# Two feed-forward stages rewritten as pipelines, and the order of work moved in one attention and in both transformers

## The chip, the cores and the metric

The kernel runs on one core of one Trainium2 chip. The metric is the device time of one execution in microseconds (us). The core has five engines that run side by side and wait for each other only through semaphores: TensorE (PE: matmuls and transposes; PEld is its weight load), VectorE (DVE), ScalarE (ACT), GpSimd (POOL) and SyncE (SP, which issues the transfers). TensorE's granted clock has two levels, 1.2 and 2.4 GHz; a granted clock of 1.00 in a row is 2.4 GHz, 0.50 is 1.2 GHz.

## The reference

`x` is 4 sequences of 512 tokens with 128 channels in float32. Four layers do

```
xn = layernorm(x);  s = attention_i(xn);  g = silu(ffn_i(xn));  x = x + s * g
```

with another attention and another feed-forward in each. Five of these eight parts are touched:

```
ffn0:  xq = fp4(xn); h = silu(xq @ fp4(Wgate).T) * (xq @ fp4(Wup).T);  y = fp4(h) @ fp4(Wdown).T     (hidden 352)
       fp4: in blocks of 16, scale = max|v| / 6, |v| / scale rounded to 0, .5, 1, 1.5, 2, 3, 4, 6, sign, * scale
attn1: 16 heads of 64, causal softmax(q k^T / 64) v, projection and bias
ffn1:  a = silu(x W1 s1) * (x W2 s2); b = gelu(a H1 s); c = gelu(b H2 s); y = c W3 s3                (hidden 512)
ffn2:  a transformer of 6 layers, 16 heads of 64, local windows of 32 keys, gated GELU of hidden 341
ffn3:  a transformer of 2 layers, 8 heads of 64, local windows of 64 keys, gated GELU of hidden 341
```

Tokens are handled in 16 tiles of 128 (TILES; four tiles, TPB, are a sequence).

## The kernel before

The program is a row of stages with a barrier of all engines between them: load, norm, attn0, ffn0, norm, attn1, ffn1, norm, attn2, ffn2, norm, attn3, ffn3, end. Inside a stage each engine has a written-out list of instructions, and the order in each list is the order of the work; nothing overtakes within an engine.

**ffn0 (`ffn0`, L1328).** One block loads the weights into `wgu` and `wd`, copies them into `src`, and rounds them: `round_fp4` (L1359) is a chain of 14 VectorE instructions, each of which waits for the one before (`step`). ScalarE first makes `mag` (absolute value) and `sgn` (sign). TensorE then transposes the rounded weights. Then a loop in hardware runs over the 4 sequences, with a barrier and a clearing of semaphores after each. In one pass everything follows in one line: copy xn to `src`, magnitude and sign, 14 steps on 512 columns, transposes, gate and up matmuls for 4 tiles with Silu and a product, magnitude and sign of 1408 columns, 14 steps on them, 12 transposes, copies, 12 matmuls of the down product, 4 copies to `u`. GpSimd only clears a tile at the start.

**attn1 (`attention1`, L1521).** 32 units (4 sequences, 8 pairs of heads). TensorE's list is `order` (L1561): for each n it holds the scores of unit n+1 (tiles 3, 2, 1, 0), between them the transposes `p` of unit n, then `weigh(n-1)` (the product of weights and values), `R(n-1)` (transposes of the reciprocal sums), the q, k and v projections of later units, and `out(n-2)`. `p`, `R`, `q`, `k`, `v` share two PSUM banks T in turn: each claims the bank that the job two before it has left (`claim`). `score(n+1, 1)` waits for the exponentials of tile 3 of the same unit, as both lie in the same banks of A. ScalarE's list (L1740) has `turned(n, 0)` ahead of `exps(n+1, 3)`.

**ffn1 (`ffn1`, L1834).** One block loads all weights and scales and waits for all ten transfers; then a hardware loop over the 4 sequences: GpSimd copies a sequence to `xb`; 8 matmuls "first" (L1885, L1886), Silu and a product; 16 matmuls "second" (L1893) and Gelu; 16 "third" and Gelu; 16 of 128 columns "last" (L1898); 4 products into `u` (L1922). A float32 matmul shows as two records.

**The transformers (`transformer`, L198).** `slots()` yields one slot for each group of 8 heads of a tile, so ffn2 (NG = 2) has 192 of them, two for a tile, and ffn3 (NG = 1) has 32, one for a tile; a slot holds work of several stages of the pipeline: `now` (attention of a group), `turn` (transposes of the next group's q and k), `ahead` (projection and norm of q, k, v), `tail` (mix the heads of a tile, and its norm), `ffn` (its gate, up, Gelu, down), `last` (its residual). For NG = 2 a slot has either `tail` and `last` or `ffn`, in turn; these are called tail slots and ffn slots below. For NG = 1 each slot has all of them. TensorE's list in a slot is: score, project q, the transpose of the norm, project k, turn p0, project v, turn p1, mix_heads, gate_up, [q here if the slot has no ffn], weigh, [q here if it has], transpose of the residual (L571), turn k, turn o, down. ScalarE's is: exponentials and squares, copy p0, copy p1, load the Gelu table, Gelu, load the Exp table, copy q (L644), copy k, copy v, copy o. The transposes and gate and up share two banks T in turn in the order of `T_list` (L235): p0, p1, gate, up, q, k, o, so q waits until Gelu has read gate, and o waits until q is copied. VectorE rotates q and k in L706 (`roped`), multiplies gate by up in L720 (`hT`), then divides the attention output (L726, L728), then norms (L680), and adds the down product to the residual in L689 at the start of the next slot. GpSimd does the powers (L398, L401) and the products of the rotation (L409 to L411).

Of the kernel before, what the change touches and what calls it, by code (L numbers as in the profile page):

```python
# [13 lines left out]
ALU = mybir.AluOpType  # L14
# [183 lines left out]
def transformer(nc, g, dram, name, depth, heads, window, hid, wqkv, qs, ks, wo, ln_g, ln_b, w1, b1, w2, b2):  # L198
# [32 lines left out]
    for now, turn, ahead, tail, ffn, last in slots():  # L231
# [10 lines left out]
    with Stage(nc, name) as st:  # L242
# [97 lines left out]
        with nc.Block() as block:  # L340
# [73 lines left out]
            def _(pe):  # L414
# [124 lines left out]
                for now, turn, ahead, tail, ffn, last in slots():  # L539
# [26 lines left out]
                    if turn is not None and ffn is not None:  # L566
                        turn_qk("q", turn)
# [12 lines left out]
            def _(act):  # L580
# [28 lines left out]

                def copy_v(n):  # L610
# [3 lines left out]
                for now, turn, ahead, tail, ffn, last in slots():  # L614
# [25 lines left out]
                    if ahead is not None and ffn is None:  # L640
                        copy_v(ahead)
                    if turn is not None:
                        t, gi = divmod(turn, NG)
                        act.activation(qT[:, turn % 2].rearrange("p j k -> p (j k)"), turned("q", turn), ACT.Copy).then_inc(T_in.sem, 1)  # L644
# [683 lines left out]
def ffn0(nc, g, d):  # L1328

    HID, BL = 352, 16  # L1330
    HC = [(c, min(P, HID - c)) for c in range(0, HID, P)]
    u, ident, xn = g["u"], g["ident"], g["xn"]
    MAXN = TPB * HID
    with Stage(nc, "f0") as st:
        wgu = st.sb("wgu", [P, 2, len(HC), DIM])
        wd = st.sb("wd", [P, HID])
        wguT = st.sb("wguT", [P, 2, HID])
        wdT = st.sb("wdT", [P, len(HC), DIM])
        src = st.sb("src", [P, MAXN])
        mag = st.sb("mag", [P, MAXN])  # L1340
        sgn = st.sb("sgn", [P, MAXN])
        acc = st.sb("acc", [P, MAXN])
        low = st.sb("low", [P, MAXN])
        scale = st.sb("scale", [P, MAXN // BL])
        inverse = st.sb("inverse", [P, MAXN // BL])
        xqT = st.sb("xqT", [P, SEQ])
        sil = st.sb("sil", [P, 2, HID])
        hqT = st.sb("hqT", [P, len(HC), SEQ])
# [1589 lines left out]
```

## Time and profile before

| | us |
|---|---|
| runs (3), median | 4454.21 (4452.24 to 4461.76) |
| the profiled execution | 4464.67 |
| its span, first to last instruction | 4463.0 |
| ffn0, from the first instruction at 301.41 to 545.62 | 244 |
| attn1, 566 to 1034.6 | 469 |
| ffn1, 1036.05 to 1230.67 | 195 |
| ffn2, about 1761 to 3834 | 2073 |
| ffn3, about 3987 to 4445 | 458 |

The rows below come from the profiled execution. Busy time of an engine is the sum of its instructions in a stretch; the text in square brackets behind a row is how long the engine had stood idle before it and what it waited for.

### The profile page before, as it was taken

The numbers are of one execution on the slowest core, as the hardware profiler recorded it, in microseconds if no ns is written. First come the engines' busy times: TensorE is split into PE (matmuls) and PEld (weight loads), VectorE is DVE, ScalarE is ACT, GpSimd is POOL, SyncE is SP. The second block draws the span as 40 slices with busy tenths as digits, with TensorE's granted clock in tenths as the row PEclk, the third lists the DMA queues.
The fourth block names the chain that finished last, engine by engine and source line by source line (L and its number), as shares of the span: only waits on it lengthen the run. The fifth ranks groups of instructions, "written<-read, shape, count | busy, mean of one in ns | idle before, by whom it ended". The sixth has DMA issues, their size and how long they took to land. (4 is left out here: it accounts for less than half of the span.)

```text
span 4463.0 us, 101112 instructions
## 1 busy us (share of the span) xinstructions
PE 3750.9 (84%) x40099; PEld 2554.7 (57%) x40109; DVE 2919.9 (65%) x6557; ACT 2452.5 (55%) x5024; POOL 2271.0 (51%) x2200
## 2 busy tenths in 40 slices
PE   7962378887879998999999999999999999658886
PEld 4542245553446564666666666666666666556665
DVE  3335544441046564888888888888888888528885
ACT  2221145552235454666766666676667667526775
POOL 1000000000012122988888888888888888227773
PEclk9975589999979898999999999999999999779998
DMA  0000000000000001211211211211211111111010
GB/s 19 2 7 0 0 21 1 1 1 27 0 7 2 1 2 34 65 39 42 62 42 40 64 39 41 66 38 42 63 41 38 42 42 38 31 49 38 21 23 20
DMA packets 103241, 128.41 MB, mean 29 GB/s; under 512 B 38232, under 2 KB 55680, under 8 KB 101888
## 3 DMA queue, kind: packets, MB, share of 16 engines
q1 hardware_dynamic: 102784, 122.05, 10.2%
q8 instruction: 320, 5.24, 0.5%
q14 instruction: 137, 1.12, 0.1%
HBM read 31.95 MB, written 3.54 MB: 8 GB/s over the span
## 5 line engine op out<-in xcount | busy, mean ns | idle before, releaser
L398 POOL TENSOR_TENSOR t_inv<-t_ssq,half 128x8 f32<-128x8 f32 x448 | 779.6, 1743 | 94.9 <-DVE t_ssq L673 75.0
L449 PE MATMUL t_wa<-t_w_qkv,t_resid 128*128 128x512 f32 x1344 | 693.3, 615 | 60.2 <-DMA t_b<-in_L_ffn_b 56.6
L409 POOL TENSOR_TENSOR t_ra<-t_qn,t_rot 128x512 f32<-128x512 f32 x448 | 569.6, 1271 | 84.5 <-DVE t_qn L680 75.8
L598 ACT ACTIVATE t_p<-t_p 128x384 f32<-128x384 f32 (+1 forms) x448 | 241.6, 539 | 498.7 <-DVE t_p L697 489.7
L706 DVE TENSOR_TENSOR t_ra<-t_ra,t_rb 128x512 f32<-128x512 f32 x448 | 314.1, 723 | 119.1 <-POOL t_rb L411 118.9
L478 PEld LDWEIGHTS t_T<-ident,t_p 128*96 128x96 f32 (+1 forms) x1792 | 192.5, 129 | 312.4 <-ACT t_p L598 280.0
L410 POOL TENSOR_TENSOR t_rb<-t_qn,t_rot 128x256 f32<-128x256 f32 x448 | 363.7, 812 | 0.0
L411 POOL TENSOR_TENSOR t_rb<-t_qn,t_rot 128x256 f32<-128x256 f32 x448 | 338.0, 754 | 0.0
L449 PEld LDWEIGHTS t_wa<-t_w_qkv,t_resid 128*128 128x128 f32 x1344 | 212.3, 192 | 178.9 <-issue 148.9
L671 DVE TENSOR_REDUCE t_ssq<-t_sq 128x8 f32<-128x512 f32 x448 | 304.9, 681 | 13.6 <-ACT t_sq L590 10.1
L486 PE MATMUL t_T<-ident,t_ra 128*128 128x128 f32 x1792 | 268.7, 278 | 42.2 <-ACT t_gg L637 32.1
L478 PE MATMUL t_T<-ident,t_p 128*96 128x128 f32 (+1 forms) x1792 | 281.5, 280 | 17.1 <-ACT t_p L598 13.8
L680 DVE TENSOR_TENSOR t_qn<-t_wa,t_inv 128x512 f32<-128x512 f32 x448 | 290.7, 684 | 4.5 <-POOL t_inv L398 4.3
L2250 POOL TENSOR_SCALAR_AFFINE_SELECT a_pt<-a_pt 128x512 f32<-128x512 f32 x128 | 80.0, 637 | 400.8 <-ACT a_pt L2234 400.8
L2257 DVE TENSOR_REDUCE a_nmax<-a_A 128x2 f32<-128x1024 f32 (+3 forms) x256 | 205.4, 823 | 117.9 <-PE a_A L2170 115.6
L695 DVE TENSOR_REDUCE t_nmax<-t_S 128x4 f32<-128x384 f32 (+1 forms) x448 | 255.4, 570 | 39.4 <-PE t_S L469 39.4
L590 ACT ACTIVATE t_sq<-t_wa 128x512 f32<-128x512 f32 x448 | 261.5, 584 | 29.3 <-PE t_wa L449 29.3
L697 DVE TENSOR_TENSOR t_p<-t_S,t_nmax 128x384 f32<-128x384 f32 (+1 forms) x448 | 258.4, 577 | 15.4
L608 ACT ACTIVATE t_pT<-t_T 96x512 f32<-96x512 f32 (+1 forms) x448 | 263.2, 588 | 3.4 <-PE t_T L478 2.7
L496 PE MATMUL t_S<-t_v,t_pT 96*64 96x66 f32 (+1 forms) x6656 | 258.2, 225 | 0.0
L2234 ACT ACTIVATE a_pt<-a_B 128x512 f32<-128x512 f32 (+1 forms) x384 | 175.9, 528 | 143.0 <-PE a_B L2181 142.9
L496 PEld LDWEIGHTS t_S<-t_v,t_pT 96*64 96x64 f32 (+1 forms) x6656 | 227.1, 137 | 36.0 <-issue 36.0
(414 smaller groups left out, 8382.2 us busy)
## 6 DMA issues: line engine op xcount, KB each, us to landing
t_v<-t_vn SPq DMA_DIRECT2D x192, 198.0 KB, 2.6
t_v<-t_vn SPq DMA_DIRECT2D x248, 132.0 KB, 2.4
t_v<-t_vn SPq DMA_DIRECT2D x144, 66.0 KB, 1.9
t_w_qkv<-in_L_ffn_Wqkv SPq DMA_DIRECT2D x6, 1536.0 KB
t_v<-t_nothing SPq DMA_DIRECT2D x48, 66.0 KB, 1.9
t_w_o<-in_L_ffn_Wo SPq DMA_DIRECT2D x6, 512.0 KB
f_h<-t_L_ffn_h_w SPq DMA_DIRECT2D x2, 1024.0 KB, 8.1
t_w<-in_L_ffn_W SPq DMA_DIRECT2D x6, 341.0 KB
```

Of the source, the lines that this page charges most:

```text
L398: pool.tensor_tensor(inv[:, n % 2, r, :], ssq[:, n % 2, r, :], g["half"][:, 0:8], ALU.pow).then_inc(inved.sem, 1)
L409: pool.tensor_tensor(ra[:, n % 2, r], qn[:, r], spread(cos, 1, 8), ALU.mult).then_inc(cosd.sem, 1)
L410: pool.tensor_tensor(rb[:, n % 2, r, :, 0:32], qn[:, r, :, 32:64], spread(sin[:, 0:32], 1, 8), ALU.mult).then_inc(sind.sem, 1)
L411: pool.tensor_tensor(rb[:, n % 2, r, :, 32:64], qn[:, r, :, 0:32], spread(sin[:, 32:64], 1, 8), ALU.mult).then_inc(sind.sem, 1)
L449: pe.matmul(bank, resid[:, b, lo:lo + P], w_qkv[:, l % 2, at:at + 512], start=True, stop=True).then_inc(wa_up.sem, 1)
L478: m = pe.transpose(bank[0:KEYS, j * P:(j + 1) * P], p[:, r, j, :], ident[:, :])
L486: m = pe.transpose(bank[:, j * P:(j + 1) * P], ra[:, n % 2, r, 2 * j:2 * j + 2, :].rearrange("p h d -> p (h d)"), ident[:, :])
L496: m = pe.matmul(S[64 * b:64 * b + 64, r, j * VD:(j + 1) * VD], pT[0:KEYS, r, j, 64 * b:64 * b + 64], windows[b][0:KEYS, 2 * j + r, :], sta ...
L608: act.activation(pT[0:KEYS, r].rearrange("p h k -> p (h k)"), turned(f"p{r}", G)[0:KEYS], ACT.Copy).then_inc(T_in.sem, 1)
L671: v.tensor_reduce(ssq[:, n % 2, r, :], sq[:, r], X, ALU.add).then_inc(summed.sem, 1)
L680: v.tensor_tensor(qn[:, r], wa[:, wa_job[kind, n] % 3, :].rearrange("p (h d) -> p h d", h=8), spread(inv[:, n % 2, r, :], 2, HD), ALU.mult ...
L706: v.tensor_tensor(ra[:, turn % 2, r], ra[:, turn % 2, r], rb[:, turn % 2, r], ALU.add).then_inc(roped.sem, 1)
```

## The change

- ffn0 is written anew as one block. All values to be rounded lie in one tile A, and are rounded in 14 parts: x0, x1, the gate and up weights, the down weights, x2, x3, and h0 to h7 of two tiles each. VectorE does seven instructions for each part, GpSimd the last two (`subtract`, and the product with the scale). ScalarE's Abs and Sign are gone. No part waits for the one before except by the order of an engine.
- ffn1 is one block without a loop. The three kinds of hidden product of two sequences are interleaved (`order`), all PSUM banks form a ring of 8, the copy to `xb` is gone, each wait for weights is only for those used, and `u` is written once for a sequence.
- attn1: `weigh(n-1)` goes from behind the last p transposes to a place behind the first two; on ScalarE `exps(n+1, 3)` goes ahead of `turned(n, 0)`.
- Transformers: in slots with ffn the transposes of q go ahead of gate and up on TensorE, with the banks in the order p0, p1, q, gate, up, k, o; the copy of q goes ahead of the Gelu table load on ScalarE. Where NG > 1 (ffn2) `down` goes ahead of `turn_o`.

```diff
@@ transformer
-        for kind, n in (("p0", now), ("p1", now), ("gate", ffn), ("up", ffn), ("q", turn), ("k", turn), ("o", now)):
+        for kind, n in (("p0", now), ("p1", now), ("q", turn), ("gate", ffn), ("up", ffn), ("k", turn), ("o", now)):
...
                         mix_heads(tail)
+                    if turn is not None:
+                        turn_qk("q", turn)
                     if ffn is not None:
                         gate_up(ffn)
-                    if turn is not None and ffn is None:
-                        turn_qk("q", turn)
                     if now is not None:
                         weigh(now, 0)
                         weigh(now, 1)
-                    if turn is not None and ffn is not None:
-                        turn_qk("q", turn)
...
                         turn_qk("k", turn)
+                    if ffn is not None and NG > 1:
+                        down(ffn)
                     if now is not None:
                         turn_o(now)
-                    if ffn is not None:
+                    if ffn is not None and NG == 1:
                         down(ffn)
@@ ScalarE
                         copy_p(now, 1)
+                    if turn is not None and ffn is not None:
+                        copy_q(turn)
                     if ffn is not None:
 
                         act.activation(spare[:, 0:1], g["half"][0:1, 0:1], ACT.Gelu)
...
                         copy_v(ahead)
+                    if turn is not None and ffn is None:
+                        copy_q(turn)
@@ ffn0, VectorE and GpSimd, for each part (lo, size)
+                    step(v.tensor_reduce(sc, blocks(src), X, ALU.max, apply_absolute_value=True))
+                    step(v.tensor_scalar(sc, sc, 1.0 / 6.0, 1e-12, ALU.mult, ALU.max))
+                    step(v.reciprocal(inv, sc))
+                    step(v.tensor_tensor(blocks(a), blocks(src), spread(inv, 2, BL), ALU.mult))
+                    step(v.tensor_scalar(c.bitcast(U32), a.bitcast(U32), 0x7F800000, None, ALU.bitwise_and))
+                    step(v.tensor_scalar(c, c, 1.0, 1.5 * 2.0 ** 22, ALU.max, ALU.mult))
+                    v.scalar_tensor_tensor(out=a, in0=a, scalar=1.0 - 2.0 ** -24, in1=c, op0=ALU.mult, op1=ALU.add).then_inc(shifted.sem, 1)
...
+                    pool.wait_ge(shifted.sem, shifted.at(k))
+                    pool.tensor_tensor(a, a, c, ALU.subtract).then_inc(lessened.sem, 1)
+                    pool.wait_ge(lessened.sem, lessened.at(k))
+                    pool.tensor_tensor(blocks(a), blocks(a), spread(scale[:, lo // BL:(lo + size) // BL], 2, BL), ALU.mult).then_inc(rounded.sem, 1)
...
+                turn_x(0)
+                turn_gu(0)
+                turn_gu(1)
+                gate_up(0)
+                turn_d()
+                turn_x(1)
+                gate_up(1)
+                for k in range(UNITS):
+                    if k in (1, 3):
+                        turn_x((k + 3) // 2)
+                    if k + 2 < UNITS:
+                        gate_up(k + 2)
+                    turn_h(k)
+                    down(k)
@@ attention1
                 order += [("p", n, 0), ("p", n, 1)]
+            if 0 <= n - 1 < UNITS:
+                order.append(("weigh", n - 1, 0))
             if 0 <= n + 1 < UNITS:
                 order.append(("score", n + 1, 1))
...
-                order += [("weigh", n - 1, 0), ("R", n - 1, 0)]
+                order.append(("R", n - 1, 0))
...
+                    if 0 <= n + 1 < UNITS:
+                        exps(n + 1, 3)
                     if 0 <= n < UNITS:
                         turned(n, 0)
                     if 0 <= n + 1 < UNITS:
-                        exps(n + 1, 3)
                         exps(n + 1, 2)
@@ ffn1
+    order = [("first", 0), ("first", 1), ("second", 0), ("second", 1), ("third", 0), ("third", 1), ("first", 2), ("last", 0),
+             ("first", 3), ("last", 1), ("second", 2), ("second", 3), ("third", 2), ("third", 3), ("last", 2), ("last", 3)]
...
+                sp.dma_start(w1[:, :], d["t_L1_ffn_w1_w"]).then_inc(w_in, 16)
+                sp.dma_start(w2[:, :], d["t_L1_ffn_w2_w"]).then_inc(w_in, 16)
                 for k, name in enumerate(("w1", "w2", "h1", "h2")):
...
+                sp.dma_start(h1[:, :, :], d["t_L1_ffn_h1_w"].rearrange("(c p) n -> p c n", p=P)).then_inc(h1_in, 16)
+                sp.dma_start(h2[:, :, :], d["t_L1_ffn_h2_w"].rearrange("(c p) n -> p c n", p=P)).then_inc(h2_in, 16)
...
+                def claim(job):
+
+                    m = job_of[job]
+                    if m >= 8:
+                        kind, b, c = jobs[m - 8]
+                        done = {"first1": silued, "first2": gated, "second": gelu1, "third": gelu2, "last": y_in}[kind]
+                        pe.wait_ge(done.sem, done.at(b, c + 1))
+                    return bank[:, m % 8, :]
...
+            @block.scalar
+            def _(act):
+                act.wait_ge(sc_in, 5 * 16)
```

## Rows read from the trace of the kernel before

**Rows 1.** Stages: stretch, its length, busy us (instructions) of each engine, PEclk, DMA, GB/s.
```profile
330.00:548.00 218.00, 65.77 (x224) 48.05 (x224) 123.37 (x148) 41.85 (x56) 0.00 (x0) 0.59 0.00 0
...
1800.00:3830.00 2030.00, 1881.42 (x21390) 1333.18 (x21390) 1691.95 (x4128) 1391.29 (x2813) 1747.96 (x1614) 1.00 0.17 46
```

**Rows 2.** Timeline of ffn0: start, length, engine, line, operation, out<-in [idle before].
```profile
301.41 0.74 POOL L1400 MEMSET f_wgu<- 128x768 f32 x1 [8.25 <-POOLq L60]
...
345.92 0.52 DVE L1466 TENSOR_TENSOR f_src<-f_sil,f_bank 128x352 f32<-128x352 f32 x1 [5.18 <-ACT f_sil L1486]
...
353.66 1.62 DVE L1374 TENSOR_REDUCE f_scale<-f_mag 128x88 f32<-128x1408 f32 x1 [2.81 <-ACT f_sgn L1489]
...
355.56 0.70 DVE L1376 RECIPROCAL f_inverse<-f_scale 128x88 f32<-128x88 f32 x1
...
357.95 0.89 DVE L1379 TENSOR_SCALAR f_acc<-f_mag 128x1408 f32<-128x1408 f32 x1
...
386.05 0.69 DVE L1374 TENSOR_REDUCE f_scale<-f_mag 128x32 f32<-128x512 f32 x1 [1.70 <-ACT f_sgn L1479]
...
545.33 0.29 DVE L1473 COPY u<-f_bank 128x128 f32 x1 [0.62 <-PE f_bank L1514]
```

**Rows 3.** Costliest groups of the page: GpSimd on 512 columns.
```profile
L409 POOL TENSOR_TENSOR t_ra<-t_qn,t_rot 128x512 f32<-128x512 f32 x448 | 569.6, 1271 | 84.5 <-DVE t_qn L680 75.8
```

**Rows 4.** Timeline of ffn2: VectorE and GpSimd at once; last, the waits of VectorE in ffn2.
```profile
2708.24 0.72 POOL L410 TENSOR_TENSOR t_rb<-t_qn,t_rot 128x256 f32<-128x256 f32 x1
...
2710.82 0.68 DVE L706 TENSOR_TENSOR t_ra<-t_ra,t_rb 128x512 f32<-128x512 f32 x1
2710.83 1.25 POOL L410 TENSOR_TENSOR t_rb<-t_qn,t_rot 128x256 f32<-128x256 f32 x1
...
DVE t_ra L706 <- POOL t_rb L411: 107.7, 91, 1.7
```

**Rows 5.** Timeline of ffn1: transfers of the scales, the fourth pass of the loop, its end.
```profile
1044.17 3.22 SPq L1871 DMA_DIRECT2D f_sc<-in_L_ffn_h_s  x2
...
1188.12 1.12 PE L1885 MATMUL f_bank<-f_xb,f_w 128*128 128x512 f32 x2 [2.55 <-POOL f_xb L1879]
...
1211.60 14.00 PE L1893 MATMUL f_bank<-f_a,f_h 128*128 128x512 f32 x32 [0.78 <-ACT f_a L1908]
...
1230.38 0.29 DVE L1922 TENSOR_TENSOR u<-f_bank,f_s 128x128 f32 x1 [0.60 <-PE f_bank L1898]
```

**Rows 6.** Timeline of attn1, TensorE: score(n+1, 1), weigh(n-1), score(n+2, 1).
```profile
790.79 0.29 PE L1656 MATMUL a_A<-a_mask,a_place 64*128 64x128 bf16 x4 [1.59 <-ACT a_p L1728]
...
793.74 2.38 PE L1682 MATMUL a_O<-a_pT,a_va 128*64 128x512 f32 x16
...
804.83 0.29 PE L1656 MATMUL a_A<-a_mask,a_place 64*128 64x128 bf16 x4 [1.59 <-ACT a_p L1728]
```

**Rows 7.** Timeline of ffn2: the start of a tail slot, and an ffn slot.
```profile
2696.97 0.73 DVE L689 SCALAR_TENSOR_TENSOR t_resid<-t_misc,t_b,t_resid 64x128 f32<-64x128 f32 x2 [0.63 <-PE t_misc L536]
...
2697.93 0.56 DVE L695 TENSOR_REDUCE t_nmax<-t_S 128x4 f32<-128x384 f32 x1 [0.22 <-PE t_S L469]
...
2711.72 0.59 ACT L608 ACTIVATE t_pT<-t_T 96x512 f32<-96x512 f32 x1
...
2716.72 0.63 PE L504 MATMUL t_T<-ident,t_o 128*128 128x128 f32 x4 [0.81 <-ACT t_qT L644]
```

**Rows 8.** Timeline of ffn3: a slot from the copy of p1 to down.
```profile
4259.18 0.61 ACT L608 ACTIVATE t_pT<-t_T 128x512 f32<-128x512 f32 x1
...
4259.77 1.49 PE L526 MATMUL t_T<-t_lnT,t_w 128*128 128x128 f32 x12
4259.81 1.28 ACT L633 ACT_TABLE_LOAD   x1
...
4261.66 0.86 DVE L720 SCALAR_TENSOR_TENSOR t_hT<-t_T,t_b,t_gg 128x128 f32<-128x128 f32 x3 [0.40 <-ACT t_gg L637]
...
4265.45 0.91 PE L536 MATMUL t_misc<-t_hT,t_w 128*128 128x128 f32 x6 [0.63 <-DVE t_ln L742]
```

More of the change, by code:

```diff
@@ L1334, in ffn0 @@
+    nth = {name: k for k, name in enumerate(parts)}
+    turns = ["x0", "gate", "up", "wd", "x1"]
+    for k in range(UNITS):
+        if k in (1, 3):
+            turns.append(f"x{(k + 3) // 2}")
+        turns += [f"h{k}a", f"h{k}b"]
+    turn_of = {name: k for k, name in enumerate(turns)}
     with Stage(nc, "f0") as st:
-        wgu = st.sb("wgu", [P, 2, len(HC), DIM])
-        wd = st.sb("wd", [P, HID])
+        A = st.sb("A", [P, COLS])
+        C = st.sb("C", [P, COLS])
+        scale = st.sb("scale", [P, COLS // BL])
+        inverse = st.sb("inverse", [P, COLS // BL])
@@ L1337, in ffn0 @@
         wguT = st.sb("wguT", [P, 2, HID])
[L1338 to L1346, printed above, removed]
+        wdT = st.sb("wdT", [P, NH, DIM])
+        xqT = st.sb("xqT", [P, BATCH, SEQ])
@@ L1521, in attention1 @@
+                    m = act.activation(wdT[0:size, c, :], wd[0:size, c * P:(c + 1) * P], ACT.Copy)
+                m.then_inc(T_in.sem, 1)
+                copy_x(1)
+                silu(1)
+                for k in range(UNITS):
+                    if k in (1, 3):
+                        copy_x((k + 3) // 2)
+                    if k + 2 < UNITS:
+                        silu(k + 2)
+                    copy_h(k)
+                    store(k)
 def attention1(nc, g, d):
@@ L1914, in _ @@
[L1914 to L1922 removed]
+                            m = pe.matmul(out[:, t * P:(t + 1) * P], a4[:, b % 2, k, t * P:(t + 1) * P], w3[:, k, :], start=(t == 0 and k == 0), stop=(k == C - 1),
+                                          skip_group_check=True)
@@ new lines, in last @@
+                    m.then_inc(up, 1)
+                for kind, b in order:
+                    if kind == "first":
+                        first(b)
+                    elif kind == "second":
+                        if b == 0:
+                            pe.wait_ge(h1_in, 16)
+                        hidden(kind, b, h1, a2, gated)
+                    elif kind == "third":
+                        if b == 0:
+                            pe.wait_ge(h2_in, 16)
+                        hidden(kind, b, h2, a3, gelu1)
+                    else:
+                        if b == 0:
+                            pe.wait_ge(w3_in, 16)
+                        last(b)
@@ new lines, in _ @@
+            @block.vector
+            def _(v):
+                v.wait_ge(sc_in, 5 * 16)
+                for kind, b in order:
+                    if kind == "first":
+                        for c in range(C):
+                            m = job_of["first2", b, c]
+                            v.wait_ge(up, m + 1)
+                            v.wait_ge(silued.sem, silued.at(b, c + 1))
+                            if b >= 2:
+                                v.wait_ge(up, job_of["second", b - 2, C - 1] + 1)
+                            v.scalar_tensor_tensor(out=a2[:, b % 2, c, :], in0=bank[:, m % 8, :], scalar=sc[:, 1, c:c + 1], in1=a1[:, b % 2, c, :],
+                                                   op0=ALU.mult, op1=ALU.mult).then_inc(gated.sem, 1)
+                    elif kind == "last":
+                        m = job_of["last", b, 0]
+                        v.wait_ge(up, m + 1)
+                        v.tensor_tensor(u[:, b * TPB:(b + 1) * TPB, :], bank[:, m % 8, :].rearrange("p (t n) -> p t n", t=TPB), spread(s3[:, :], 1, TPB),
```

402 lines of the change are left out of this document (203 added, 199 removed).

## The prediction, made before the changed kernel was run

> **What bounds the kernel now.** I read the table of stages first, then a timeline of each touched stage, then the waits. The stages run one after the other, so each change is worth what its own stage loses or gains. Three kinds of stage are seen. ffn0 is a single line: no engine is busy for even 60% of it, TensorE is at a mean granted clock of 0.59, and GpSimd does nothing [rows 1]; there the sum of the chain counts. ffn2 is tight: TensorE 93%, GpSimd 86%, VectorE 83% of its stretch at clock 1.00 [rows 1]; there only what ends last in a slot counts. In attn1 and ffn1 TensorE is nearly always busy at full clock, and its holes are what can be won [rows 5, 6].
>
> **ffn0.** The stage lasts from 301.41 to 545.62, 244.2 us [rows 2]. New VectorE time: an instruction on two or one source takes 0.69 us on 512 columns and 1.62 on 1408, so 0.89 on 704; a constant operation 0.89 on 1408, so about 0.53 on 704 and 0.43 on 512; the reciprocal 0.70 on 1408, so 0.42; the product 0.52 a tile [rows 2]. A part h is 3 x 0.89 + 2 x 0.53 + 0.42 + 0.2 (blocks' scale) + 0.2 of gaps = 4.55, and 1.1 for its two products: 5.65. An x part is 3.65, the gate and up weights (768) 4.8, the down weights (352) 2.95. Sum: 4 x 3.65 + 4.8 + 2.95 + 8 x 5.65 = 67.6 us. The two GpSimd instructions of a part take 1.27 us each on 512 columns [rows 3], by columns 1.75 each on 704. Can they run beside VectorE? In ffn2 a VectorE sum of two SBUF tensors started at 2710.82 for 0.68, and the GpSimd product that started at 2710.83 took 1.25 instead of 0.72 [rows 4]: it stood still for about as long as they overlapped. I take it that this holds both ways. Then GpSimd's 3.6 us for part k must fit beside what VectorE does at the start of part k+1 from PSUM or as a reduction and reciprocal: 2.7 us for an h part, so VectorE stands 0.9 for each of h1 to h7 (6.3), and 1.3, 0.9, 2.7, 0.5, 1.3 at the five parts behind x0 (6.7). 67.6 + 13.0 = 80.6, and the tail (GpSimd 3.6, six transposes and their copies 1.9, six matmuls 1.3, the store, hand-overs) is 7.5. So 88 us, 156 less. Whether the new bitwise operation runs at the constant operation's rate is not in the trace: at the slower rate it is 0.36 x 14 = 5 us more. TensorE has 4.3 us in an h part at full clock (8 records of 352 columns at 0.30, scaled from 14.00 us for 32 of 512 [rows 5], 6 transposes, 12 short records), below 6.6; the transfers of weights are hidden by x0 and x1, which wait for nothing. Bounds: 169 less without any blocking, 135 less if TensorE stays slow and blocking is dearer.
>
> The Trainium skill states the same blocking as a rule (SBUF — State Buffer, "Who interferes with whom"): a VectorE instruction with two SBUF inputs, or in a two-port mode, shares one port pair with GpSimd and whoever is second waits for the whole of the other. It speaks against dividing a rounding chain between these two engines. By that rule the 13 us above are lost; without it they are not, and the row above agrees with it in one direction.
>
> **ffn1.** A float32 record of 512 columns is 14.00 / 32, about 0.43 us at full clock [rows 5]. A sequence has 80 of them (34.4) and 32 short ones of 0.11 (3.5): 37.9, four 151.6. Before, the holes are the barrier and copy of each pass, 2.55 [rows 5], the wait for the last product ahead of "second", and the load of all weights. Now TensorE begins when w1 and w2 are in, near 1040, fills eight banks (16 records, 6.9 us, about 5 us of it at the low clock) and then waits for ScalarE, which waits for the scales. Their slow issues (3.22 for the last two, ending at 1047.39 [rows 5]) now stand ahead of three weight issues, some 2 us earlier: landed at 1048.5, table and first Silu until 1050.5. The end is 1050.5 + 151.6 - 6.9 = 1195.2, with the last product 1196.1, against 1230.67 [rows 5]: 35 less. Bounds 30 and 38: a stall at the Gelu and Silu table changes is covered by the eight banks, and if h1 landed late the cost is a few us once.
>
> **attn1.** A unit takes 804.83 - 790.79 = 14.04 us. In each, score(n+1, 1) waits 1.6 to 1.8 us for exponentials, and weigh, 2.3 us, comes later [rows 6]. Put ahead, weigh fills the hole. What is late next: R(n-1) stood behind weigh, and now stands right behind the last transposes, whose bank must be copied; by ScalarE's order (turned 2, exps 1, turned 4) I find it 0.3 late, and k then waits 0.1 for the copy of R. Exps 3 ahead of turned 0 gives ScalarE an earlier start and costs nothing, since p2 comes after weigh. Net 1.8 - 0.3 = 1.5 a unit, times 30 full units: 45 less. Bounds 25 (R and k late by 1 us together) and 55 (nothing late).
>
> **ffn2.** Only ffn slots change, 95 or so. TensorE now turns q right behind p1. Its input is L706, ready at 2711.50 [rows 4], when p1 ends; its result comes 0.63 later [rows 7], just as ScalarE ends the copy of p1 (2711.72 + 0.59 = 2712.31 [rows 7]). The copy of q then stands ahead of the Gelu table load and moves Gelu, `hT` and the divisions by 0.51. In return o no longer waits 0.81 for the copy of q [rows 7], and down, ahead of o, is done before VectorE wants it: the waits of 0.63 in L689 and 0.22 in front of the first maximum of the next slot [rows 7] go. Gain 0.85 - 0.51 = 0.34. But when GpSimd gets in first, L706 ends 0.6 later: then its next wait for GpSimd is 0.69 instead of 1.37, and 107.7 us over 91 waits, 1.18 each [rows 4], say that this is so in 0.27 of the slots. There ScalarE now stands 0.6. That takes 0.16. GpSimd starts its next products about 0.9 later, which its slack in the tail slot holds, though L706 there may meet it: up to 0.3, I take 0.03. So 0.15 x 95, 14 less. Bounds: 37 less (never late) and 40 more (always late, and a collision in the tail slot).
>
> **ffn3.** Here mix_heads stands between p1 and q, so q starts only when gate did, at 4259.77, and ScalarE, done with p1 at 4259.79 [rows 8], waits 0.6 for it, copies 0.57, and loads the Gelu table at 4261.0 instead of 4259.81. The whole slot hangs on Gelu: `hT` waits for it (0.40), and down waits 0.63 for the norm behind it [rows 8]. What the move saves, the wait of o, was not on this path, and down isn't moved here. So 1.18 a slot over 30 slots: 35 more. Bounds: 0 and 40.
>
> **Sum.** -156 - 35 - 45 - 14 + 35 = -215. Against the profiled execution, 4464.67, that is 4250. The median of the runs is 10.5 lower, so 4239, said as 4240.
>
> **Rivals.**
> A. The transformer order pays, or costs nothing, in ffn3 too (a slack that I read wrongly; the banks freed earlier let gate and up finish sooner). For it: o waits less; against it: the one-line chain through Gelu. Then 4240 - 35 - 20 = 4185 to 4205.
> B. ffn2 turns slower: L706 comes late in most ffn slots, since the hand-over is a matter of 0.01 us [rows 4], and ScalarE stands ahead of Gelu. 0.34 - 0.6 - 0.15 is 0.4 lost a slot: 4240 + 14 + 39 = 4293.
> C. ffn0 with TensorE at the low clock, as it is on average now [rows 1]: 8.6 us an h part instead of 6.6: 4256. Against it, it would then be busy all the time, and in ffn1 it keeps the full clock over a hole of 2.55 [rows 5].
> D. No blocking between VectorE and GpSimd: 4227. By the skill's rule on the port pair, named above, this cannot be; the rows show the one direction only.
> E. Slower than before: the shift of GpSimd in ffn2 makes all four L706 of each pair of slots lose a GpSimd instruction, 0.7 each, with nothing to hide it: 2.8 x 96 = 269, 4509. It decides from 2.2 us lost a pair; the slack of GpSimd in the tail slot speaks against it.
>
> **How the numbers follow.** The forecast 0.50, with its own range 4215 to 4265; A 0.17, B 0.17, C 0.06, D 0.09, E 0.01. The predicted time is the forecast's, 4240. The range takes in most of A and B and the bounds of ffn0 and attn1: 4190 to 4290. A difference of 0.2% (9 us) is what the runs can tell from none; 200 us of ffn0 and attn1 alone are far over it: faster 0.98, same 0.01, slower 0.01.
>
> **What would show it.** ffn0: its last instruction 88 us after its first, an h part every 6.6 us, with GpSimd instructions or VectorE's products stretched where they meet, TensorE's clock near 1; a period of 5.7 means D, over 8 means C. ffn1: 160 us, "second" without a hole. attn1: a period of 12.5, the wait of score(n+1, 1) gone, a small one in front of R. ffn2: no wait in L689, pairs of slots at 20.9 instead of 21.1. ffn3: a wait of ScalarE for q of 0.6 ahead of the table load, slots at 13.9 instead of 12.7. The forecast is wrong if the stages' gains don't add up to 200 to 240, above all if ffn3 isn't slower.

## The result, and the profile after

The changed kernel takes 4262.2 us (median of 4 runs, 4251.6 to 4265.5) against 4453.2 (4447.5 to 4461.8) for the kernel before, run on the same chip: a ratio of 0.9565, 95% interval 0.9543 to 0.9588. The profiled execution took 4263.45, with a span of 4261.4. The forecast was 4240, its range 4190 to 4290.

The stages, each from its first instruction or transfer issue to its last instruction in the two profiled executions, beside the forecast:

| stage | before | after | difference | forecast |
|---|---|---|---|---|
| ffn0 | 244.2 | 84.8 | -159 | -156 |
| attn1 | 468.1 | 425.1 | -43 | -45 |
| ffn1 | 194.6 | 158.8 | -36 | -35 |
| ffn2 | 2075.7 | 2056.9 | -19 | -14 |
| ffn3 | 459.3 | 520.4 | **+61** | +35 |
| the rest | | | -6 | 0 |

Four terms came within 5 us. The fifth is off by 26, and is the subject of half of the experiments. The first view is the table of stretches of the kernel after, the same view as [rows 1] (its columns: stretch, length, busy us and instructions of PE, PEld, DVE, ACT and POOL, granted clock, DMA share, GB/s):

```profile
301.40:387.00 85.60, 52.61 (x233) 36.86 (x233) 72.86 (x114) 22.49 (x50) 39.33 (x30) 0.76 0.03 7
387.00:831.00 444.00, 404.59 (x2768) 230.44 (x2768) 215.60 (x376) 243.66 (x721) 29.31 (x40) 0.96 0.02 6
831.00:992.00 161.00, 154.85 (x448) 76.27 (x448) 14.65 (x21) 37.89 (x52) 0.00 (x0) 0.98 0.06 19
1519.80:3575.00 2055.20, 1903.76 (x21516) 1342.06 (x21517) 1778.16 (x4166) 1414.28 (x2837) 1777.01 (x1636) 0.99 0.18 48
3725.40:4245.00 519.60, 420.76 (x3920) 301.01 (x3920) 350.54 (x878) 313.32 (x607) 304.67 (x292) 0.88 0.10 25
```

In ffn0 VectorE is now busy for 85% of the stretch. In ffn1 TensorE is busy for 154.85 of 161. The last row is ffn3: its granted clock is 0.88, and in the kernel before the same view gives it 0.94:

```profile
3987.60:4445.50 457.90, 378.48 (x3917) 276.95 (x3918) 350.69 (x878) 308.77 (x606) 305.21 (x292) 0.94 0.12 29
```

VectorE and GpSimd do the same work in the same busy time in both. TensorE has the same instructions too (3920 against 3917 records) and is busy for 42 us more: its instructions have become longer. So a part of the stage's loss is clock.

ffn0, where [rows 2] showed a single line of work. The timeline of one h part after the change, VectorE and GpSimd:

```profile
347.52 1.68 POOL L1442 TENSOR_TENSOR f_A<-f_A,f_C 128x704 f32<-128x704 f32 x1 [2.88 <-DVE f_A L1431]
348.34 0.89 DVE L1425 TENSOR_REDUCE f_scale<-f_A 128x44 f32<-128x704 f32 x1
349.28 1.41 POOL L1444 TENSOR_TENSOR f_A<-f_A,f_scale 128x704 f32<-128x704 f32 x1
349.48 0.43 DVE L1427 RECIPROCAL f_inverse<-f_scale 128x44 f32<-128x44 f32 x1
349.94 1.50 DVE L1428 TENSOR_TENSOR f_A<-f_A,f_inverse 128x704 f32<-128x704 f32 x1
351.48 0.53 DVE L1429 TENSOR_SCALAR f_C<-f_A 128x704 uint32<-128x704 uint32 x1
```

GpSimd's second instruction runs from 349.28 to 350.69, and VectorE's product (L1428), which starts at 349.94, takes 1.50 where the same instruction in part h0, with GpSimd idle, takes 0.89. The reduction at 348.34 ran beside GpSimd at its full speed, as forecast. The bitwise operation took 0.53, the constant operation's rate. L1428 starts at 343.90, 349.94, 355.99, 362.03: a period of 6.04.

attn1, TensorE in one unit, the counterpart of [rows 6]:

```profile
597.85 0.29 PE L1709 MATMUL a_A<-a_mask,a_place 64*128 64x128 bf16 x4
601.17 0.63 PE L1744 MATMUL a_T<-ident,a_rep 128*128 128x128 f32 x4 [0.30 <-ACT a_pT L1791]
608.26 2.38 PE L1735 MATMUL a_O<-a_pT,a_va 128*64 128x512 f32 x16
610.56 0.28 PE L1709 MATMUL a_A<-a_mask,a_place 64*128 64x128 bf16 x4
```

The score rows stand right behind weigh, without a wait, 12.71 apart instead of 14.04. The transposes of R wait 0.30, the size named ahead.

ffn1, against [rows 5]: the issue of two scales, the first matmuls, the first Silu and the last instruction.

```profile
834.38 1.43 SPq L1936 DMA_DIRECT2D f_sc<-in_L_ffn_h_s  x2
835.76 14.81 PE L1958 MATMUL f_bank<-xnT,f_w 128*128 128x512 f32 x27 [5.43 <-DMA f_w<-t_L_ffn_w_w]
841.04 1.26 ACT L2004 ACTIVATE f_a<-f_bank,f_sc 128x512 f32<-128x512 f32 x2 [1.83 <-DMA f_s<-in_L_ffn_w_s]
990.65 0.69 DVE L2036 TENSOR_TENSOR u<-f_bank,f_s 128x512 f32<-128x512 f32 x1 [2.88 <-PE f_bank L1974]
```

The issue of those two scales takes 1.43 where it took 3.22 in [rows 5]. Silu starts 8.5 us after the stage's first issue, and TensorE never waits for it: from 835.76 on it is busy nearly without a hole.

ffn2, tail slot then ffn slot, against [rows 4, 7]:

```profile
2511.29 0.72 DVE L695 SCALAR_TENSOR_TENSOR t_resid<-t_misc,t_b,t_resid 64x128 f32<-64x128 f32 x2
2524.93 0.68 DVE L712 TENSOR_TENSOR t_ra<-t_ra,t_rb 128x512 f32<-128x512 f32 x1
2524.95 1.25 POOL L410 TENSOR_TENSOR t_rb<-t_qn,t_rot 128x256 f32<-128x256 f32 x1
2526.36 0.60 ACT L611 ACTIVATE t_qT<-t_T 128x512 f32<-128x512 f32 x1
2526.97 1.28 ACT L638 ACT_TABLE_LOAD   x1
```

The wait of 0.63 ahead of the residual is gone, and the copy of q (L611) stands between the copy of p1 and the table load without a wait, when L712 was on time. A pair of slots lasts 20.61. In 30 of 95 pairs it lasts 0.6 more or somewhat longer (21.2 to 21.6); in each of these the L712 ahead of the ffn slot took 1.3, as GpSimd had come first. The forecast had taken 0.27 of them.

ffn3, one slot at full clock, then down and the residual of another slot:

```profile
3899.27 0.60 ACT L611 ACTIVATE t_qT<-t_T 128x512 f32<-128x512 f32 x1 [0.62 <-PE t_T L486]
3899.88 1.28 ACT L638 ACT_TABLE_LOAD   x1
3903.74 0.66 PE L504 MATMUL t_T<-ident,t_o 128*128 128x128 f32 x4 [0.84 <-DVE t_o L734]
3905.52 0.91 PE L536 MATMUL t_misc<-t_hT,t_w 128*128 128x128 f32 x6 [1.12 <-DVE t_ln L748]
...
4037.11 1.62 PE L536 MATMUL t_misc<-t_hT,t_w 128*128 128x128 f32 x6 [1.12 <-DVE t_ln L748]
4038.77 0.73 DVE L695 SCALAR_TENSOR_TENSOR t_resid<-t_misc,t_b,t_resid 64x128 f32<-64x128 f32 x2 [1.21 <-PE t_misc L536]
```

The first two rows are the step as forecast: ScalarE waits 0.62 for q behind mix_heads, copies it, and loads the table 1.2 us later. TensorE stands 1.12 ahead of down, which was 0.63 in [rows 8]. The last two are what was not forecast: the same six matmuls in 1.62 instead of 0.91. Slots last 13.92 when all records are short, but 15 of the 26 inside the two layers last 14.65 to 16.43, with spells of low clock. Together these 15 are 24.7 us longer than 15 slots of 13.92.

### The profile page after: what moved, and what is told of

The parts are those of the page before. It is cut to its first block and busy times, and to the rows that moved or that the text cites. A ratio compares the mean times of both kernels' runs of the same rounds, so it can differ in the third digit from the quotient of the medians.

```text
span 4261.4 us, 100713 instructions
## 1 busy us (share of the span) xinstructions
PE 3769.6 (88%) x40109; PEld 2559.2 (60%) x40109; DVE 2916.9 (68%) x6495; ACT 2433.3 (57%) x5007; POOL 2308.9 (54%) x2225
## 3 DMA queue, kind: packets, MB, share of 16 engines
q14 instruction: 137, 1.12, 0.1%
## 5 line engine op out<-in xcount | busy, mean ns | idle before, releaser
L449 PE MATMUL t_wa<-t_w_qkv,t_resid 128*128 128x512 f32 x1344 | 702.6, 622 | 61.4 <-DMA t_b<-in_L_ffn_b 58.2
L712 DVE TENSOR_TENSOR t_ra<-t_ra,t_rb 128x512 f32<-128x512 f32 x448 | 365.5, 835 | 123.9 <-POOL t_rb L411 123.9
L486 PE MATMUL t_T<-ident,t_ra 128*128 128x128 f32 x1792 | 279.0, 278 | 65.3 <-DVE t_ra L712 36.8
L486 PEld LDWEIGHTS t_T<-ident,t_ra 128*128 128x128 f32 x1792 | 199.2, 141 | 108.1 <-DVE t_ra L712 70.3
```

Source lines behind the costliest of these rows:

```text
L449: pe.matmul(bank, resid[:, b, lo:lo + P], w_qkv[:, l % 2, at:at + 512], start=True, stop=True).then_inc(wa_up.sem, 1)
L486: m = pe.transpose(bank[:, j * P:(j + 1) * P], ra[:, n % 2, r, 2 * j:2 * j + 2, :].rearrange("p h d -> p (h d)"), ident[:, :])
L712: v.tensor_tensor(ra[:, turn % 2, r], ra[:, turn % 2, r], rb[:, turn % 2, r], ALU.add).then_inc(roped.sem, 1)
```

## The experiments

Times of stages are from each kernel's profiled execution, from first to last instruction. "Slot" is the distance between two residual updates, in ffn2 "pair" the same for an ffn slot and a tail slot together. "All pairs" leaves out those at the ends of layers, which are 1 to 2 us longer in every kernel. Ratios are to the kernel before, run beside them.

**1. q in its old place in ffn3 alone, and in both transformers.** `early` is false where q is turned and copied in its old place.

```diff
-    (transformer, all)
+    early = NG > 1          # first kernel; second kernel: False, and down behind turn_o again
+    if turn is not None and not early and ffn is not None: turn_qk("q", turn)      # behind weigh
+    if turn is not None and (ffn is None or not early): copy_q(turn)               # behind Gelu and the Exp load
```

> The changed kernel, but in ffn3 (NG == 1) the transposes and the copy of q stand where they stood before. Theory (the order of q makes ScalarE load the Gelu table 1.2 us later a slot, and the longer idle of TensorE then lets its granted clock fall in some slots; both are gone with the order): ffn3 back to 457 us from 518, the kernel at 4262 - 61 = 4201, granted clock of the stage 0.94 instead of 0.88, no slot of 15.8 us or more but the first. Rival 1 (the clock fell for a reason outside the order, for instance because the stages ahead are now denser): the slots of 12.72 come back but some stay long, ffn3 480 to 485, the kernel 4225 to 4230. Rival 2 (ffn3's 61 us come from something else in the change that both transformers share): ffn3 stays over 500.

Measured: 4190.8 (0.9418, 0.9400 to 0.9436). ffn3 454.3, clock 0.96, slots 12.71. The order of q carries the whole loss of ffn3 and more (66 instead of 61; the stage of the kernel before had a clock of 0.94).

> The changed kernel with all edits of the transformers undone in both of them; ffn0, attn1 and ffn1 as changed. Theory (in ffn2 the order pays 19 us, in ffn3 it costs 61): ffn2 at 2071 to 2073 us instead of 2053, ffn3 at 457, the kernel at 4262 + 19 - 61 = 4220, and 19 slower than the kernel with only ffn3 in the old order. Rival (ffn2's 19 us are variation between runs, or come from elsewhere): ffn2 stays near 2053, the kernel at 4201, equal to the one with only ffn3 in the old order.

Measured: 4220.5 (0.9476, 0.9459 to 0.9492). ffn3 456.7; ffn2 2075.8, all pairs 21.07: the two edits together are worth 19 to 27 us there (the stage was 2048.5 to 2057.3 in the six kernels that have them as changed, by how often L712 was late).

**2. Is it the clock? Filling TensorE's holes, and moving q further ahead.**

```diff
+    for j in range(4): pe.transpose(bank[:, j * P:(j + 1) * P], ident[:, :], ident[:, :])    # ahead of the wait for o
+    for j in range(6): pe.transpose(S[...], ident[:, :], ident[:, :])                        # ahead of down's wait
```

> The changed kernel, with transposes of the identity whose results nobody reads in two holes of TensorE in ffn3: 4 in o's bank ahead of the wait for the attention output (0.66 us in a hole of 0.84), 6 in the score bank ahead of down's wait for the norm (about 0.95 in a hole of 1.12). Theory (the long slots of 15.8 to 16.4 us are the granted clock, which falls since TensorE stands idle longer): the clock of ffn3 goes from 0.88 to 0.95 or more, nearly all slots are 13.9, ffn3 at 30 x 13.93 + about 70 = 490 instead of 518, the kernel near 4235. Rival 1 (long slots come from a late transfer or from GpSimd, and the low clock is only how the stand shows): the added work changes nothing or adds up to 10 us: 4262 to 4272. Rival 2 (the clock falls for the sum of a longer stretch, and two short fillings don't reach it): fewer long slots, 4240 to 4255.

Measured: 4227.3 (0.9490, 0.9474 to 0.9506). Nearly every slot is 13.86, ffn3 487.9, clock 0.96:

```profile
3724.80:4211.00 486.20, 424.05 (x4230) 309.04 (x4231) 350.48 (x878) 311.32 (x606) 304.97 (x292) 0.96 0.11 27
```

This kernel does *more* work in the same order and gains 32 us in the stage: the long slots were the clock, and it held once most of TensorE's idle time was filled.

```diff
+    if turn is not None and NG == 1: turn_qk("q", turn)      # ahead of mix_heads
     if tail is not None: mix_heads(tail)
```

> The changed kernel, with the transposes of q in ffn3 right behind those of p1, ahead of mix_heads. Theory (of the 1.2 us that a slot lost at full clock, 0.6 is ScalarE's wait for q behind mix_heads and 0.6 the copy itself): ScalarE's wait of 0.6 to 0.7 in front of the copy of q is gone or below 0.2, but gate now comes 0.6 later on TensorE only if it has no slack there, which it has, since Gelu waits for the table: slots at full clock 13.3 to 13.4, ffn3 18 us less by that, and fewer long slots: 490 to 500, the kernel 4235 to 4245. Rival (VectorE's sum over y, which waits for mix_heads, moves back by 0.6 and with it the norm on which down waits): slots stay at 13.9, the kernel 4262.

Measured: 4218.9 (0.9475, 0.9459 to 0.9491). Slots 13.60, ffn3 483.0, no long slot but at the layer's end. The direction held, the size did not: ScalarE still waits 0.29 for q, because the transposes now wait 0.35 for VectorE's rotation. So 12.72 + 0.60 + 0.29 = 13.61. In the changed kernel the same sum is 12.72 + 0.60 + 0.62 = 13.94, measured 13.92. The clock held, though TensorE's idle time in a slot is nearly that of the changed kernel (2.13 against 2.22).

**3. Each edit of a pair alone, in ffn2 and attn1.** Both kernels have ffn3 in the old order.

```diff
-    if ffn is not None and NG > 1: down(ffn)       # ffn2, ahead of turn_o; now behind it
-    exps(n + 1, 3); turned(n, 0)                   # attn1, ScalarE
+    turned(n, 0); exps(n + 1, 3)
```

> Against the kernel with ffn3 in the old order (4190.8 us; ffn2 2050.3, attn1 445). ffn2: only the q edit is kept, down stands behind o again. attn1: only the move of weigh is kept, ScalarE's list is the old one. Theory for ffn2 (the gain of the pair of edits is down's place; q early only saves o a wait which the copy of q, 0.6 ahead of Gelu, gives back): pairs of slots at 21.05 to 21.1 with some 0.6 longer, ffn2 2075 to 2095. Rival (q early is what pays, since o stops waiting): pairs at 20.7, ffn2 about 2055. Theory for attn1 (weigh in the hole is the whole gain): a unit stays at 12.7 us, attn1 within 5 us of 445. Rival (without ScalarE's edit the exponentials of tile 3 are late and the score waits come back): 13.0 to 13.3 a unit, 10 to 20 us more. Kernel: 4216 to 4236 by the theories, 4195 to 4215 by the rivals.

Measured: 4253.6 (0.9538, 0.9513 to 0.9562). ffn2 2102.5: pairs at 21.11, and 33 of 95 at 21.7. With q early alone the stage is **27 us slower than before**, more than either number allowed. The waits of TensorE say why; the columns are the total, the number and the longest:

```profile
PE t_T L506 <- DVE t_o L736: 76.1, 92, 1.0
```

That is 0.83 each time: o waits as long as it did before, only for VectorE's output now, which Gelu has delayed, instead of for the copy of q. attn1 425.2: weigh alone is the whole gain. (The 445 that the text above starts from is not the stage's time in that kernel: it took 427.3 there.)

```diff
+    early = False                                  # ffn2: q in its old place, down ahead of turn_o
-    order.append(("weigh", n - 1, 0))              # attn1, TensorE, behind p0 and p1
+    order += [("weigh", n - 1, 0), ("R", n - 1, 0)]
```

> Against the kernel with ffn3 in the old order (4190.8 us; ffn2 2050.3, attn1 445). ffn2: only down goes ahead of o; q is turned and copied where it was. attn1: only ScalarE's edit is kept, weigh stands behind the last p transposes again. Theory for ffn2: down (0.83) fills the 0.81 for which o waited, the scores of the next slot start 0.54 earlier, VectorE's waits of 0.63 and 0.22 go, nothing is put ahead of Gelu, and a late rotation of q delays nobody: all pairs at 20.5, ffn2 2075.7 - 96 x 0.56 = 2022, better than with both edits. Rival (both are needed, hT is not ready when down wants it): pairs at 20.9 or more, ffn2 2060 to 2075. Theory for attn1: score(n+1, 1) waits 1.6 to 1.8 again, a unit at 13.9 to 14.04, attn1 about 40 to 44 more: 485 to 489. Rival (ScalarE's edit itself shortens the wait): 13.4, 465 to 470. Kernel: 4190.8 - 28 + 42 = 4205 by the theories.

Measured: 4180.7 (0.9376, 0.9357 to 0.9395). ffn2 **2014.0**, all pairs 20.4: down alone is worth 62 us, two to three times what both edits are worth. The timeline of an ffn slot:

```profile
2512.14 1.18 PE L488 MATMUL t_T<-ident,t_ra 128*128 128x128 f32 x8 [0.34 <-ACT t_gg L646]
2513.16 0.83 PE L538 MATMUL t_misc<-t_hT,t_w 128*128 128x128 f32 x6
2513.42 0.57 ACT L615 ACTIVATE t_qT<-t_T 128x512 f32<-128x512 f32 x1
2514.13 0.63 PE L506 MATMUL t_T<-ident,t_o 128*128 128x128 f32 x4
```

Down fills the 0.81 of [rows 7] exactly: while it runs, ScalarE copies q, and o follows without a wait. attn1 449.2, a unit of 13.42: the rival was right by its period (its 465 to 470 started from the same 445), ScalarE's edit alone shortens the score's wait from 1.59 to 0.98. With weigh in the hole it adds nothing.

**4. ffn0's last two operations on VectorE.**

```diff
-    GpSimd: pool.tensor_tensor(a, a, c, ALU.subtract); pool.tensor_tensor(blocks(a), blocks(a), spread(scale...), ALU.mult)
+    VectorE: step(v.tensor_tensor(a, a, c, ALU.subtract)); v.tensor_tensor(blocks(a), blocks(a), spread(sc, 2, BL), ALU.mult)
```

> Against the kernel with ffn3 in the old order (4190.8 us; ffn0 85 us, a part h every 6.05). ffn0: the subtraction and the product with the scale go from GpSimd to VectorE, nothing else. Theory (the product with the inverse scale takes 1.50 instead of 0.89 because GpSimd's product runs at its start, and the limit at its start 0.71 instead of 0.19 in part x1 for the same reason): both go back to 0.89 and 0.19; a part h takes 6.05 - 0.61 + 2 x 0.89 + 0.05 = 7.25, the stage 97 us, the kernel 4203. Rival (1.50 is what that product takes by its operands, whatever GpSimd does): a part h 7.85, the stage 102 to 106.

Measured: 4211.4 (0.9453, 0.9434 to 0.9472), ffn0 94.7. Its timeline, the limit and the product with the inverse in parts h0 to h2:

```profile
334.15 0.19 DVE L1430 TENSOR_SCALAR f_scale<-f_scale 128x44 f32<-128x44 f32 x1
...
342.12 0.89 DVE L1432 TENSOR_TENSOR f_A<-f_A,f_inverse 128x704 f32<-128x704 f32 x1
...
349.42 0.89 DVE L1432 TENSOR_TENSOR f_A<-f_A,f_inverse 128x704 f32<-128x704 f32 x1
```

1.50 is back to 0.89 with GpSimd silent, and the limit of h0 is 0.19 (0.71 in the changed kernel): the blocking of VectorE by GpSimd is shown, in the direction that the rows of before did not have. It costs 0.6 a part, the division saves 1.8: a part h takes 7.30 instead of 6.04.

**5. The table load ahead of the copy of q in ffn2; ffn1 sequence by sequence.** ffn3 in the old order.

```diff
+    act.activation(spare[:, 0:1], ..., ACT.Gelu); copy_q(turn)                       # ScalarE, ffn2
+    gate_up(ffn, gate alone); weigh(now, 0); weigh(now, 1); gate_up(ffn, up alone)   # TensorE, ffn2
+    order = [(kind, b) for b in range(BATCH) for kind in ("first", "second", "third", "last")]   # ffn1
```

> Against the kernel with ffn3 in the old order (4190.8 us; ffn2 2050.3, ffn1 160). ffn2: ScalarE loads the Gelu table ahead of the copy of q, and TensorE puts weigh between gate and up, since up's bank is that of q. Theory (pairs of 21.2 come from the copy of q waiting for a rotation that GpSimd made 0.6 late, and the table load of 1.3 hides that): no pairs at 21.2, but up ends up to 0.4 later: pairs at 20.6 to 20.9, all alike, ffn2 2040 to 2060. Rival (the long pairs come from the extra 0.6 of VectorE itself): pairs of 21.2 stay in a third. ffn1: the products go sequence by sequence in place of the interleaved order; one block, ring of banks and loads stay. Theory: second and third wait for the last Gelu or product ahead of them as in the loop of before (0.78 at each), three times in each of four sequences: 9 us more, 169, with the clock held. Rival (the interleaving carries most of the 36 us, since TensorE's clock falls in the holes): 180 or more.

Measured: 4254.1 (0.9537, 0.9517 to 0.9558). ffn2 2104.2, outside both numbers. Pairs are nearly alike (21.29 to 21.42), although 34 of the rotations were late: their 0.6 does vanish, behind the load as the theory had it or behind the wait below. But all of them are 0.7 longer:

```profile
DVE t_hT L732 <- PE t_T L528: 90.3, 87, 1.2
```

VectorE waits 1.04 for up, put behind weigh; 0.4 was expected. ffn1 163.3, where 169 was expected: interleaving is worth 4.5 us of the 36 (6 against the kernel with ffn3 in the old order, whose ffn1 took 157.4). The single block, the dropped copies and the loads awaited one by one make up the rest; they were not tried apart.

**6. Only what pays.** q in its old place in both transformers, down ahead of o in ffn2, all else as changed.

```diff
+    early = False          # in both transformers; the rest is the changed kernel
```

> The changed kernel with q in its old place in both transformers and down ahead of o in ffn2; ffn0, ffn1 and both edits of attn1 as changed. Theory (the parts add up, since the stages are apart): ffn2 2014 and ffn3 455 as in the kernel with down only, attn1 425 as in the changed kernel in place of 449: 4180.7 - 24 = 4157. Rival (TensorE's clock in a later stage depends on how dense the earlier ones were, so that gains are partly given back): 4165 to 4180.

Measured: 4162.2 (5 runs, 4153.9 to 4165.4; 0.9335, 0.9317 to 0.9353), 100 us less than the changed kernel. ffn2 and ffn3:

```profile
1526.40:3538.00 2011.60, 1899.78 (x21515) 1341.91 (x21516) 1742.57 (x4166) 1407.56 (x2837) 1779.28 (x1636) 0.99 0.18 49
3690.50:4143.00 452.50, 375.12 (x3916) 273.74 (x3917) 351.04 (x878) 308.37 (x606) 305.24 (x292) 0.96 0.12 29
```

ffn2 2013.7, ffn3 454.4: the parts add up.

**7. The suspected cost by itself: copies that nobody reads.**

```diff
+    for k in range(2 if NG == 1 else 1): act.activation(unread[:, k], xnT[:, 0:512], ACT.Copy)   # ahead of the Gelu load
```

> The kernel with only what pays, and ahead of each load of the Gelu table ScalarE makes copies of 512 columns that nobody reads: one in ffn2 (0.6 us), two in ffn3 (1.2 us). No order is changed. Theory for ffn3 (all of the 61 us that the change lost there comes from ScalarE reaching the table load 1.2 us later: 36 directly, the rest through the granted clock, which falls once the slot is 13.9 long): slots of 13.9 mixed with slots of 15.8 to 16.4, low clock for about 120 us of the stage, ffn3 510 to 520. Rival (the clock fell because of the order of TensorE's work, not of its idle time): all slots 13.9, ffn3 about 490. Theory for ffn2 (the copy of q ahead of Gelu costs 0.2 a pair, the rest of what q early loses is its waiting for a late rotation): all pairs at 20.6, no 21.2 among them, ffn2 2014 + 19 = 2033. Rival (moving Gelu by 0.6 is the whole loss, lateness comes with it): pairs of 21.2 among them, ffn2 2050. Kernel: by the theories e9 + 60 + 19.

Measured: 4235.1 (0.9504, 0.9485 to 0.9523). ffn2 2061.2, above both numbers: all pairs 20.91, 0.51 more than 20.40, and no late ones (one of 21.25, at a place that is longer in every kernel). A copy ahead of Gelu costs 0.51, nearly the whole of its record of 0.63, and not 0.2; q early costs only 0.21 a pair in the on-time pairs, so 0.3 comes back elsewhere; where was not tried. The late pairs come only with q early. ffn3: slots 13.74, ffn3 484.9, and the clock held, the rival's sign:

```profile
3732.30:4215.00 482.70, 375.67 (x3914) 272.77 (x3915) 351.00 (x878) 340.32 (x670) 305.03 (x292) 0.95 0.11 27
```

Read as it stands, order mattered and idle time did not. But 13.74 was less than the 13.92 wanted, so the next two kernels went further from either side.

```diff
-    for k in range(2 if NG == 1 else 1):
+    for k in range(3 if NG == 1 else 0):
```

> The kernel with only what pays (4162; ffn3 454, slots 12.72), with three copies of 512 columns that nobody reads ahead of the Gelu table load in ffn3, none in ffn2. With two of them a slot was 13.74, TensorE idle 2.51 us in it, in three holes (0.84 ahead of q, 0.79 ahead of o, 0.60 ahead of down) spread over 4.1 us, and the clock held; in the changed kernel 2.28 in two holes (0.84 ahead of o, 1.09 ahead of down) within 2.6 us, and it fell. Theory 1 (idle time counts by how close together it lies): the third copy lengthens the hole ahead of q to 1.35 and leaves the two later ones; the slot is 14.25 with 3.0 us idle, more than in the changed kernel, and the clock still holds: ffn3 500, the kernel 4207. Theory 2 (the whole idle time or the length of a slot decides, with a bound that 13.74 just misses): slots of 16 us among them, ffn3 525 or more, the kernel over 4230.

Measured: 4223.9 (0.9475, 0.9453 to 0.9497). ffn3 524.8: slots 14.25 for three slots, and then 14.97 and 15.7 in turn to the end of the stage.

```profile
3689.50:4212.00 522.50, 409.83 (x3913) 298.25 (x3914) 351.26 (x878) 360.48 (x701) 304.80 (x292) 0.88 0.10 25
```

Theory 1 fell, and the stage time of theory 2 (525 or more) was met. TensorE's order is that of the fast kernel here, nothing but idle time was added, which also makes the slots longer, and the clock fell to the 0.88 of the changed kernel.

The other one is the changed kernel with the first of the two fillings of experiment 2.

```diff
+    for j in range(4): pe.transpose(bank[:, j * P:(j + 1) * P], ident[:, :], ident[:, :])    # ahead of the wait for o alone
```

> The changed kernel, with 4 transposes of the identity that nobody reads in ffn3 in the hole ahead of o alone; the one of 1.09 ahead of down stays open. Theory 1 (two holes close together make the clock fall): with 0.4 + 1.09 left, as in the kernel with q ahead of mix_heads (0.51 + 1.09), the clock holds, slots 13.86 to 13.93, ffn3 488, the kernel 4230. Theory 2 (the single hole of 1.1 is what makes it fall, as it lies at the end of the slot): slots of 15.8 and 16.4 stay, ffn3 510 or more.

Measured: 4235.3 (0.9510, 0.9493 to 0.9531). ffn3 494.8, slots 13.92, but four inside the stage at 15.1, each with a spell of low clock. Theory 2 fell, and theory 1 is met only in part: one hole less makes the falls rare, not absent. The kernels side by side; idle time is that with no record on TensorE in one slot at full clock, long slots are counted among the 26 inside the two layers:

| kernel | slot | idle | long slots |
|---|---|---|---|
| q in its old place | 12.71 | 1.49 | none |
| q ahead of mix_heads | 13.60 | 2.13 | none |
| two copies | 13.74 | 2.47 | none |
| both holes filled | 13.86 | 1.04 | none |
| first hole filled | 13.92 | 1.78 | 4 |
| the changed kernel | 13.92 | 2.22 | 15 |
| three copies | 14.25 | 3.00 | all behind the third |

The sum of idle time doesn't rank them, nor does the closeness of the holes. The length of the slot does, and no run holds it fixed while the clock goes from never falling to falling. So it is shown that the added wait brings the clock down (three copies) and, at the same slot of 13.92, that less idle time makes the falls fewer (first hole filled); how idle time and the slot's length work together stays open. The Trainium skill (TensorE: Matmul & The Clock Gate, "A second HAM failure mode: psum-queue depth-cycling") tells of a kernel whose short idle times between groups of matmuls made the clock swing between its two levels; the trace agrees, with single holes of 1.12 us at most.

## Why the prediction was right, and the step that failed

- **What bounds, and stages add up:** right. The parts of the total were separable to a few us in all kernels. The profiled executions differ by 201 us where the sum had 215: the 26 us missed in ffn3 are partly hidden by 3 to 6 us more than forecast in ffn0, in ffn2 and between the stages, which is luck and no part of the sum. The other 8 of the 22 us between 4240 and 4262 are the 10.5 taken off for the median: after the change the profiled execution is only 1.2 above it.
- **ffn0, 88 us:** 84.8. An h part took 6.04 where the forecast had 6.6: GpSimd's second instruction takes 1.41, not the 1.75 scaled from [rows 3], so VectorE stood still 0.6 instead of 0.9 a part, and its own work took 5.4 instead of 5.65. The mechanism is shown by experiment 4. The Trainium skill's rule (SBUF — State Buffer, "Who interferes with whom") agrees with it in both directions here. What the prediction drew from it, that it speaks against dividing the chain, does not hold in this case, since the division gained 10 us net of the blocking. Rival C, TensorE at the low clock through the h parts, did not come: it needed a period of 8.6.
- **ffn1, 35 less:** 36 less, but not by the start that was forecast. The scales were taken to hold up the first Silu until 14.5 us after the stage's first issue, with TensorE waiting on full banks. Silu started at 8.5, and TensorE never waited for it. Its own work, taken as 151.6, kept it busy for 154.85, as the first records ran at the low clock. The two errors, 4.3 us and 3.3 us, nearly cancel: that the size came out so close is luck.
- **attn1, 45 less:** 43 less, the mechanism right. The unit is 12.71 and not 12.5: the wait that went is the 1.59 of [rows 6], where the sum had 1.8. That ScalarE's edit "costs nothing" held; that it alone would bring 19 us was not seen, and with weigh moved it brings none.
- **ffn2, 14 less:** 19 to 27 less. The late rotations were sized nearly right (0.27 forecast, 0.16 to 0.32 measured in the six kernels). What the prediction missed is that it costed two edits as one, "in return o no longer waits 0.81 for the copy of q, and down, ahead of o, is done". Down alone fills that 0.81, for nothing. q early alone does not: o then waits 0.83 for VectorE, which the copy ahead of Gelu delays. Separately the edits are worth -62 and +27, together -19 to -27.
- **ffn3, 35 more:** 61 more. This is the step that was mis-sized: "1.18 a slot over 30 slots: 35 more. Bounds: 0 and 40". The 1.2 us at full clock are right (13.92 against 12.72, 36 us). The other 25 are TensorE's clock, which fell in the longer slots with their longer holes: the 15 long slots have 24.7 of them, and with the holes filled the stage is 32 us shorter. The upper bound was wrong for that reason: the cost of a delay on the path was bounded by its own length. [Rows 1] has the clock of ffn0 and ffn2 only; ffn3's was not weighed, and rival C looked for a clock effect in ffn0 alone.
- **Rivals:** A and B are ruled out by the stage times (A: ffn3 slower; B: ffn2 faster), C by ffn0's period, D by the 1.50 of L1428. E's premise, that GpSimd blocks more rotations, came true: 108 of VectorE's rotations of q take 1.3 instead of 0.7 in the changed kernel, 25 in the kernel before. But 75 of the 108 lie in the tail slots and lengthen no pair, and without q early none costs anything: with down alone 102 are blocked, and all pairs last 20.4.

## What to carry to other kernels

When two edits are aimed at one hole, cost each alone: one may have all of the gain and the other only its price. Work put ahead of a table load on the engine that the slot hangs on costs nearly its whole length (0.51 for a copy of 0.63). And where a change lengthens TensorE's waits, bound its price beyond the delay itself, by what the same records take at the lower clock; a few idle transposes in the hole are a cheap test, and here nearly half the cure.

## What the hardware did that was not expected

- Slots of 13.60 kept the full clock, slots of 13.92 with the same work lost it in more than every second one. In the low spells down takes 1.62 instead of 0.91.
- Once fallen, the clock can lock into a pattern: with three idle copies there was a low spell in every pair of slots (14.97 and 15.7) to the end of the stage.
- GpSimd also holds up short VectorE instructions on SBUF: in part h0 of ffn0 the limit on 44 columns took 0.71 instead of 0.19 while GpSimd's product of part x3 ran (the expectation of experiment 4 names part x1).

```profile
330.81 1.06 POOL L1444 TENSOR_TENSOR f_A<-f_A,f_scale 128x512 f32<-128x512 f32 x1
331.20 0.71 DVE L1426 TENSOR_SCALAR f_scale<-f_scale 128x44 f32<-128x44 f32 x1
```
